# A linear-attention stage: constant products ahead of PE's waits, a router bias moved out of its loop, and state steps one step later

## The reference, cut to what matters

```python
def step(S, inp):
    rt, dt, kt, vt, at, bt = inp
    sa = jnp.einsum('bhij,bhj->bhi', S, at)
    S = S * dt[:, :, None, :] + sa[..., None] * bt[:, :, None, :] + vt[..., None] * kt[:, :, None, :]
    y = jnp.einsum('bhij,bhj->bhi', S, rt)
    return (S, y)
...
y = (yh.reshape(B_ * T_, C_) * ln_w + ln_b).reshape(B_, T_, C_)      # yh: y, normed per head
y = y + ((rr * kr * time_faaaa).sum(-1, keepdims=True) * vr).reshape(B_, T_, C_)
x = x + y * g @ w_output.T
...
confidences = jax.nn.sigmoid(jnp.einsum('bsh,eh->bse', x, conf_w) + conf_b)
bids = confidences * wealth
top_bids, selected_experts = jax.lax.top_k(bids, K)
```

## Time and profile before

| | us |
|---|---|
| median of 3 runs | 4253.3 (4241.2 to 4257.55) |
| the profiled execution's own time | 4258.15 |
| its span, first to last instruction | 4256.4 |

### The profile page before, as it was taken

One profiled execution on the slowest core, in us unless ns is written; L12 is line 12 of the kernel. 1 busy time (PEld: TensorE's weight loads), 2 busy tenths in 40 slices (PEclk: granted clock), 3 DMA queues, 4 the chain that ended last, 5 costly groups with the idle time before them and its releaser, 6 DMA issues.

```text
span 4256.4 us, 69444 instructions
## 1 busy us (share of the span) xinstructions
PE 3484.6 (82%) x28042; PEld 2414.7 (57%) x28042; DVE 2805.6 (66%) x5367; ACT 1893.8 (44%) x3124; POOL 860.2 (20%) x907
## 2 busy tenths in 40 slices
PE   7999999975388989847888888888888888859995
PEld 4555555533255555525566566666666666648774
DVE  4666666633289889837777766666677676637775
ACT  3444444341377887724333333344333333216652
POOL 0003000002411221122221212222221221114553
PEclk7999999985699999969898898888888888859997
DMA  9997000001122122020000000000000000016666
GB/s 169 162 160 218 1 1 1 1 13 49 42 63 69 55 69 67 13 63 1 6 6 2 6 6 6 6 6 6 6 6 1 6 6 6 6 45 218 219 226 179
DMA packets 208113, 233.52 MB, mean 55 GB/s; under 512 B 12189, under 2 KB 182431, under 8 KB 201392
## 3 DMA queue, kind: packets, MB, share of 16 engines
q1 hardware_dynamic: 193712, 203.62, 20.0%
q0 software_dynamic: 14080, 25.45, 1.8%
HBM read 136.19 MB, written 96.48 MB: 55 GB/s over the span
## 4 chain that ended last, share of the span: by engine, by line
PE 54%; DVE 24%; ACT 11%; issue 7%; DMA 2%; SPq 1%; POOL 1%; another core or an unknown queue 0%; DVEq 0%; POOLq 0%; ACTq 0%
DVE t L2095 6%; PE ps L1501 5%; PE ps L1559 4%; PE ps L134 4%; PE ps L136 3%; PE ps L135 3%; PE ps L1591 3%; DVE t L477 2%; PE ps L1597 2%; PE ps L1600 2%; PE ps L852 2%; PE ps L333 2%; ACT t L979 2%; ACT t L977 2%; PE ps L859 1%
## 5 line engine op out<-in xcount | busy, mean ns | idle before, releaser
L2095 DVE COPY_PREDICATED t<-t,ps 128x512 f32<-128x512 uint32 x384 | 349.0, 909 | 102.9 <-PE ps L1559 96.0
L1501 PE MATMUL ps<-t 128*128 128x512 f32 x608 | 344.5, 679 | 33.1 <-DVE t L1961 15.0
L1871 ACT ACTIVATE t<-ps 128x512 f32<-128x512 f32 (+1 forms) x256 | 139.1, 544 | 511.5 <-PE ps L1600 401.9
L477 DVE TENSOR_REDUCE t<-ps 128x2 f32<-128x512 f32 (+1 forms) x512 | 260.7, 551 | 120.1 <-PE ps L292 119.9
L416 ACT ACTIVATE t<-ps 128x768 f32<-128x768 f32 x256 | 207.5, 811 | 252.5 <-PE ps L321 251.9
L134 PE MATMUL ps<-t 128*128 128x512 f32 (+1 forms) x660 | 279.7, 424 | 42.3 <-DVE t L503 25.8
L1591 PE MATMUL ps<-t 128*128 128x128 f32 x1280 | 242.7, 317 | 59.2 <-ACT t L1871 28.0
L1591 PEld LDWEIGHTS ps<-t 128*128 128x128 f32 x1280 | 199.6, 214 | 148.2 <-issue 85.4
L1559 PE MATMUL ps<-t 64*128 64x128 f32 x3072 | 239.8, 299 | 25.9 <-DVE t L2067 25.7
L136 PE MATMUL ps<-t 128*128 128x512 f32 (+1 forms) x660 | 258.8, 392 | 0.0
L135 PE MATMUL ps<-t 128*128 128x512 f32 (+1 forms) x660 | 258.6, 392 | 0.0
(11 more groups left out here) (424 smaller groups left out, 8744.8 us busy)
## 6 DMA issues: line engine op xcount, KB each, us to landing
t<-experts SPq DMA_DIRECT2D x39, 1536.0 KB
sorted<-t SPq DMA_DIRECT2D x4, 10855.0 KB, 145.9
t<-in_wP SPq DMA_DIRECT2D x92, 320.5 KB
experts<-t SPq DMA_DIRECT2D x8, 1536.0 KB, 6.1
t<-sorted SPq DMA_DIRECT2D x39, 260.0 KB
t<-answers SPq DMA_DIRECT2D x16, 512.0 KB, 6.7
t<-in_wE SPq DMA_DIRECT2D x8, 768.0 KB, 7.7
paired<-t SPq DMA_DIRECT2D x1, 6026.0 KB, 47.9
```

What stands on the lines that cost most here:

```text
L477: m = dve.e.tensor_reduce(nmf[:, z, blk * 16 + 4 * g + i0:blk * 16 + 4 * g + i0 + 2], ps[:, k:k + 2, a0:a1], AX.X, ALU.max, negate=True)
L1501: pe.e.matmul(ps[out, k, :], lhs, rhs, start=True, stop=True).then_inc(*e_pe(u, name))
L2095: dve.e.copy_predicated(out, msk.bitcast(U32), src).then_inc(*i_dve(k, "lev", li))
```

## The change

A function `hold(k, n)` issues one product of the constants `w["bones"]` (128 x 128) and the first n columns of `w["masks"]` into bank k of PSUM, where the next product writes over it. It is called at the transposes (n = 128), and with n = 256 at "q", at "bd", at "s" of each state step, at "fc", at the router's logits and at its ranks. At these places PE first waits for the bank to be free, then does the constant product, and then waits for the data. The bias of the four logit tiles becomes one product of 32 columns, ahead of the wait for the data, with the bias written four times in `cbias`; the four products with the weights add to it. On all engines the S steps come one step later: S has 27 steps, and step 0 holds only the copy of the first state on DVE.

```diff
@@ -1336,14 +1336,14 @@
-               ("cw", 128, 8), ("cbias", 128, 8), ("ones", 128, 128), ("wealth", 128, 8), ("desc", 128, 8),
+               ("cw", 128, 8), ("cbias", 128, 32), ("ones", 128, 128), ("wealth", 128, 8), ("desc", 128, 8),
...
-STEPS = {"E": 29, "L": 17, "I": 12, "S": 26}
+STEPS = {"E": 29, "L": 17, "I": 12, "S": 27}
 PACE = {"E": 0.8, "L": 0.9, "S": 0.8}
-WRITTEN = 15
+WRITTEN = 16
...
+        def hold(k, n):
+
+            pe.e.matmul(ps[:, k, 0:n], w["bones"], w["masks"][:, 0:n], start=True, stop=True, skip_group_check=True)
...
                 b = misc.take("tp", k)
                 pe.wait_ge(*misc.free("tp", k))
+                hold(b, 128)
...
                 b = misc.take("q", k)
+                pe.wait_ge(*misc.free("q", k))
+                hold(b, 256)
                 pe.wait_ge(i_dve, k, "ap", 4)
-                pe.wait_ge(*misc.free("q", k))
...
                 bk = [b1, b1 + 1, b2, b2 + 1]
+                hold(b1, 256)
...
         def state(u, s):
-            z = u % 2
-            if s <= 6:
+            z, s = u % 2, s - 1
+            if 0 <= s <= 6:
                 ck = s + 1
                 cur = Sx[:, s % 3, :, :]
+                if ck < 7:
+                    k = misc.take("s", u, ck)
+                    pe.wait_ge(*misc.free("s", u, ck))
+                    hold(k, 256)
                 pe.wait_ge(s_dve, u, "S", s)
...
                 k = misc.take("fc", u)
+                pe.wait_ge(*misc.free("fc", u))
+                hold(k, 256)
                 pe.wait_ge(s_dve, u, "rk")
...
                 k = misc.take("rl", u)
+                pe.wait_ge(*misc.free("rl", u))
+                hold(k, 256)
+                pe.e.matmul(ps[:, k, 0:32], w["ones"], w["cbias"], start=True, stop=False, skip_group_check=True)
                 pe.wait_ge(r_dve, u, "xn")
-                pe.wait_ge(*misc.free("rl", u))
                 for j in range(4):
-                    out = ps[:, k, j * 8:j * 8 + 8]
-                    pe.e.matmul(out, fin[2][:, j * 128:j * 128 + 128], w["cw"], start=(j == 0), stop=False,
-                                skip_group_check=True)
-                    m = pe.e.matmul(out, w["ones"], w["cbias"], start=False, stop=True, skip_group_check=True)
+                    m = pe.e.matmul(ps[:, k, j * 8:j * 8 + 8], fin[2][:, j * 128:j * 128 + 128], w["cw"], start=False,
+                                    stop=True, skip_group_check=True)
...
                 k = misc.take("rk", u)
+                pe.wait_ge(*misc.free("rk", u))
+                hold(k, 256)
                 pe.wait_ge(r_dve, u, "prior")
-                pe.wait_ge(*misc.free("rk", u))
...
         def state(u, s):
+            s -= 1
             if s == 9:
...
-            if s <= 6:
+            s -= 1
+            if s < 0:
+                dve.wait_ge(i_act, 4 * u + 3, "bd")
+                if u:
+                    dve.wait_ge(s_pe, u - 1, "y", 7, 1)
+                dve.e.tensor_copy(Sx[:, 0, :, :], BN[:, z, 0, :, 64:128]).then_inc(*s_dve(u, "S", 0))
+            elif s <= 6:
```

More of the change, by code:

```diff
@@ L1633, in state @@
         def state(u, s):
-            z = u % 2
-            if s <= 6:
+            z, s = u % 2, s - 1
+            if 0 <= s <= 6:
                 ck = s + 1
                 cur = Sx[:, s % 3, :, :]
+                if ck < 7:
+                    k = misc.take("s", u, ck)
+                    pe.wait_ge(*misc.free("s", u, ck))
+                    hold(k, 256)
                 pe.wait_ge(s_dve, u, "S", s)
                 if ck < 7:
-                    k = misc.take("s", u, ck)
                     pe.wait_ge(i_act, 4 * u + 3, "bd")
-                    pe.wait_ge(*misc.free("s", u, ck))
                     for b in range(2):
@@ L1659, in state @@
                 k = misc.take("fc", u)
+                pe.wait_ge(*misc.free("fc", u))
+                hold(k, 256)
                 pe.wait_ge(s_dve, u, "rk")
-                pe.wait_ge(*misc.free("fc", u))
                 pe.e.matmul(ps[:, k, :], w["bones"], fin[2], start=True, stop=True).then_inc(*s_pe(u, "fc"))
@@ L2117, in state @@
             gv = G[:, z3, :].rearrange("p (b c) -> p b c", b=2)
-            if s <= 6:
+            s -= 1
[5 more added lines that the diff above has]
+            elif s <= 6:
                 ck = s + 1
                 cur, nxt = Sx[:, s % 3, :, :], Sx[:, ck % 3, :, :]
-                if s == 0:
-                    dve.wait_ge(i_act, 4 * u + 3, "bd")
-                    if u:
-                        dve.wait_ge(s_pe, u - 1, "y", 7, 1)
-                    dve.e.tensor_copy(cur, BN[:, z, 0, :, 64:128]).then_inc(*s_dve(u, "S", 0))
                 if ck < 7:
@@ L2406, in pack_c @@
     place = np.arange(2)[None, :, None] * NT + np.arange(64)[None, None, :] * 128 + i[:, None, None]
-    p.update(cw=g("conf_w").T, cbias=np.concatenate([g("conf_b")[None], z(127, 8)], 0),
+    p.update(cw=g("conf_w").T, cbias=np.concatenate([np.tile(g("conf_b"), 4)[None], z(127, 32)], 0),
              ones=np.ones((128, 128), np.float32), wealth=every(g("wealth")), desc=every(np.arange(8, 0, -1)),
```

## The result

The changed kernel took 4225.94 us (median of 7 runs, 4218.47 to 4238.56), the kernel before 4257.39 (4241.2 to 4270.47, 7 runs): a ratio of 0.9932 with a 95% interval of 0.991 to 0.9953, 31 us in place of the 125 forecast. The profiled execution took 4227.96 us, its span 4226.2.

A forecast was written before the change was run, and what follows sets the result against it. Stage C was taken as bound by DVE and a low-clocked PE in turn; -9.1 clock, -0.9 logits, -2.0 waits and +3.7 products gave -8.3 us a unit, -125 over 15, 3 back in the tail: 4130 us, range 4055 to 4278.

The forecast's parts named there:

- the signs: Stage C: higher clock, unit of 110 to 113 us, first-state wait gone, DVE's chain share above 24%.
- The wait at the first state: PE's wait before the state products goes, as they come one step behind the copy; -2.0 us a unit.
- the first sign: Granted clock over stage C of 0.93 or more in place of 0.85.
- the sum: Per unit of stage C: -9.1 - 0.9 - 2.0 + 3.7 = -8.3 us, times 15 is -125 us.
- what the clock gives back: Five low-clock stretches of a unit: 15.2 us saved on PE, 0.6 of it on the path, -9.1 us.
- the back and forth: Within a unit: DVE full and PE starved, clock falls, then PE slow and DVE idle half of the time.
- my own working of "q" and of the logits: PE's gaps shrink: at "q" from 2.60 to 1.5 us, at the logits from 1.83 to about 0.4.
- the price of the products: 21 constant products a unit: 8.4 us of PE work, 6.1 exposed, +3.7 us on the path.
- The falls one by one: Clock falls at logits, "q", first state and fc go; the one at "sq" counts half, gap near 2.0 us.
- the second rival: Constant products don't hold PE's clock and add exposed work: +2.8 us a unit, 4295 us, slower; chance 0.13.
- The tests: Stage C: clock 0.84 to 0.87 with PE busier, products fail; clock near 1, unit above 115 us, DVE took over.
- rival one: DVE takes over; falls go only at logits and first state: -2.8 us a unit, 4211 us; chance 0.21.

The follow-up runs named there:

- moved kernel: Changed kernel with a unit's eight scatters issued at the next unit's first eight state steps: 4161.93 us, 0.9795 of the kernel before (4246.07 us).
- second series: Against the kernel before (4244.54 us): changed kernel again 0.9959, without constant products 0.9896, with them only at "q", fc and logits 0.9955.
- first series: Against the kernel before (4189.62 us): order alone 0.9773, constant products alone 0.9893; scatters moved in the changed kernel 0.9832, in the kernel before 0.991.

## Why the prediction was right and wrong

**Right: the direction, and part of the signs.** The wait at the first state went, the logits' and fc's gaps went and took their falls with them, and the low clock of the unit fell from 37.5 us to 17.0. But the first sign asked for 0.93 over the stage, and that is 0.91 (0.93 is the unit's); the unit was to take 110 to 113 us and takes 116; and DVE's share of the chain stayed at 24%.

**Wrong, the main step: the sum has no late signals.** The -8.3 us a unit are added up from gaps, clock and products, and nothing in them is time in which a product is done and its signal isn't out. I read "DVE is idle half of the time" as PE being slow at the low clock. In the second low stretch of the earlier trace rows, DVE's idle time is this wait for "n":

```profile
2836.92 0.69 DVE L1994 TENSOR_SCALAR t<-ps 128x512 f32<-128x512 f32 x1 [7.37 <-PE ps L1501]
```

Part of it is what I took it for: "n" itself ends only at 2836.9. Part is late signals: PE's products of "q" (L1613) and of the chunk's step 4 (L1576) had ended by 2831.2, and their signals came together at 2832.85. How much is late signals shows in the kernel before with moved scatters, where none is late: DVE waits 3.8 us for "n" on average (45.1 / 12) in place of 5.9, so about a third.

```profile
DVE t L1994 <- PE ps L1501: 45.1, 12, 4.6
```

With the new order the signals of "bd" and "n", for which ACT and DVE stand still, fall into the middle of the row in place of its end, and PE stops for 6.1 us, ACT for 7.4 and DVE for 9.2. Between series with and without it the changed kernel differs by 4226.2 - 4106.0 = 120 us of span. The units account for that: 9.0 us in each of some eleven is 99, and 19.7 more come in the last two. The kernel before differs by 45 to 68 us (4244 to 4257 against 4190 to 4199). So the late signals cost the new order some 60 to 80 us more than the old one. Where the signals are in time, the change gave 101 us of the 125 forecast; where they are late, 13 to 31. That the signals are late because of the row is shown by three pairs, each within one series that has late signals (the changed kernel with its row moved, and in two fours, and the version without products moved) and by the last units of the moved kernel. The row alone isn't enough: in two series the same row of eight holds nothing. How it holds PE's signals stays open. That landings are missing from the records in just those traces points at the way that signals, or their records, take. Every time here is of an execution whose clock and spans were recorded, so no run tells whether a launch without records has late signals.

**Wrong: who brings the clock back.** I booked 9.1 us a unit as what the clock gives back, by order and products together, and had the constant products "break the second half" of the back and forth, as if the falls stayed without them. The runs say otherwise. Without a single constant product the clock of the unit was 0.94 where no signal was late, and the time 0.9722; with all of them 0.95 and 0.9765. In the second series a unit has some 31 us of low clock in the kernel before, 22 with the order and the router's bias, and 17 with the products too. So the larger part goes because the order no longer stops PE, as my own working of "q" and of the logits half said: their gaps shrink by the order as much as by the products. Alone, the products do raise the clock (0.9893 in the first series); together with the order they have little left to raise.

**Wrong: the price of the products.** Estimated at 8.4 us of work a unit, 3.7 on the path. L1500 is busy for 213.2 us over 16 units, 13.3 us a unit (672 records, two to a product); from each one's start to the next product's, idle time left out, the 21 of the unit take 11.7 us. One of 256 columns takes 0.44 to 0.64 us in that way at full clock, most often 0.53, and 1.15 at the low one (0.63 from 2856.05 to 2856.68 in the timeline above), where I had taken 0.44 from two neighbours of 128 columns. On the path the products cost 1.7 us a unit net of the clock that they give back (116.05 against 114.35 with late signals; 107.05 against 105.4, the mean of nine units, without). The prediction never set their own share of the 9.1 us against their 3.7.

```profile
L1500 PE MATMUL ps<-t 128*128 128x256 f32 (+1 forms) x672 | 213.2, 401 | 8.5 <-DVE t L1978 7.5
```

**The falls one by one.** Four were to go and the one at "sq" to stay by half. Logits, first state and fc: right. At "q" I expected 1.3 us to be left and 1.77 is. That gap alone is no fall in the first trace after: the fall comes 10 us later, inside the 6.10 us. At "sq" 1.80 us are left (about 2.0 expected), but no fall starts there; the last stretch begins at 2867.90, 1.3 us after a gap of 1.29 us ended. That is shorter than the 1.47 us under which I had counted a fall as gone, and "q" keeps its clock behind a longer one: the length of one gap doesn't decide it. The count of falls was nearly right, and the longest of the gaps isn't one that I had priced.

**The Trainium skill's rule.** "TensorE: Matmul & The Clock Gate", section "HAM oscillation — how this bites in real kernels", would have no fall go by filling gaps as short as these. The traces stand against it again: three of five falls went with gaps of 1.83 to 2.8 us, the last one left has no gap over 1.80 us in the 30 us ahead of it, and the second rival (4295 us, slower) didn't come. The fall inside the gap of 6.10 us is one that agrees with the page.

**The tests were ambiguous.** A clock near 1 with a unit above 115 us was to say that DVE took over, with longer waits of PE for L2117, L2153 and L2165. The unit is 116 us, PE waits for L2117 up to 6.1 us, and the time lies near rival one's (4211 us). Yet the clock is 0.93, PE's waits for L2153 are what they were for L2140 (37.7 and 37.0 us from 1850 to 3780), and those for L2165 are gone (0.7 in place of 41.7). And DVE is busy for 81.5 us of 116.07, less than before, and idles for 9.2 at the very place. The long wait for L2117 ends a chain whose head is PE's own signal. The time agreed with that rival and its mechanism did not.

## What to carry to other kernels

Before you book an engine's idle time as the price of a slow partner, look at when the partner's work ended: a wait that ends microseconds after it, at the same moment on two engines, is a late signal and no slow engine, and an edit of the order can move critical signals into its stretch. Break up rows of indirect transfers: a row moved and broken into two fours was worth 1.6 to 1.8% in the series with late signals, and cost some 0.7% in one without. And read the trace for what was issued when: one transfer to each step in the code came out as two rows of four. Order first, then fillers: constant products pay only where the order leaves gaps, and here the version without them and with moved scatters was the fastest in both series that had late signals and it ran in (0.9676 and 0.9718); where the signals were in time, the one without products and with the row of eight was (0.9722).

## What the runs showed of the hardware that was not expected

- PE's signals were recorded up to 7.3 us (9.7 in the last units) after their products started while POOL issued eight indirect transfers in 10 us, and came out together 1.5 us after the last was issued. Two rows of four left 1.5 to 3.3 us (4.1 once), and two rows with 1.3 us of other work between them 1.6 to 3.9.
- In the same traces over 40% of the scatters' landings are missing from the semaphore records (694 to 1196 of 2048 are there); in the others at most 10 of 2048.
- The same kernel shows this in some series and not in others: 4226, 4231 and 4230 us with it, 4098 without. What sets it for a series stays open; the chip's number doesn't. Two versions compared in different series would have been ranked wrongly by more than this change is worth.
- PE's clock fell behind a gap of 6.10 us, and it didn't behind 1.77 and 1.80 us, while another fall came 1.3 us behind a gap of 1.29; in the kernel before, gaps of 1.83 us and more had a fall behind them.
